# Row panel sums of the first sweep: added by VectorE, or carried on in PSUM from a copy by ScalarE

## What is computed

```python
d = rsqrt(sum(adj, axis=1) + 1e-6)
x = layernorm(x + (d[:, None] * (adj + I) * d[None, :]) @ (x @ W0))      # layer 0
agg = adj @ x                                                             # layer 1
msg = relu(agg @ W_msg.T + b_msg)
x = layernorm(x + gru_cell(msg, x, W_ih, W_hh, b_ih, b_hh))
```

## Time and profile before

| | us |
|---|---|
| median of 3 runs | 1845.35 |
| lowest and highest | 1844.21, 1848.05 |
| profiled execution, its time | 1845.82 |
| its span in the trace | 1844.0 |
| first sweep, to the end of its last product | about 713 |

### The profile page before, as it was taken

The page is one execution under the profiler, slowest core; times in us unless marked ns, Lnnn a source line. Parts: engine busy times, 40 slices in busy tenths (PEclk is TensorE's granted clock), DMA queues, the critical chain, the costliest instruction groups (busy, mean ns, idle before and its releaser), DMA issues.

```text
span 1844.0 us, 16697 instructions
## 1 busy us (share of the span) xinstructions
PE 1696.3 (92%) x6400; PEld 1160.4 (63%) x6400; DVE 1444.7 (78%) x1346; ACT 641.9 (35%) x560; POOL 117.0 (6%) x110
## 2 busy tenths in 40 slices
PE   0088799997999999999999999999999999999996
PEld 0043344443444556888888888888777777777774
DVE  7888899999999966766666655665877888878785
ACT  0000000000000003445454444444665666566562
POOL 0000000000000011200000000000001011110101
PEclk9999999999999999999999999999999999999998
DMA  9999999999999962666566565665998888989891
GB/s 390 422 386 422 420 423 420 421 416 422 384 422 421 420 236 85 205 196 202 195 197 201 192 201 191 198 196 188 384 314 303 299 302 309 311 291 319 286 313 51
DMA packets 180927, 551.10 MB, mean 299 GB/s; under 512 B 13424, under 2 KB 13936, under 8 KB 148080
## 3 DMA queue, kind: packets, MB, share of 16 engines
q1 hardware_dynamic: 177280, 541.11, 79.4%
q0 software_dynamic: 2560, 8.39, 1.3%
q10 hardware_dynamic: 1008, 0.53, 0.1%
HBM read 545.79 MB, written 4.19 MB: 298 GB/s over the span
## 4 chain that ended last, share of the span: by engine, by line
PE 76%; DVE 12%; DMA 9%; issue 2%; ACT 1%; POOL 0%; SPq 0%; DVEq 0%; ACTq 0%; POOLq 0%
PE bank L487 17%; PE bank L489 17%; PE bank L488 17%; PE bank L435 15%; DMA ring<-adj_blocks 6%; DVE colsum L763 5%; DVE feat L767 2%; DVE feat L770 2%; DMA pool<-adj_blocks 2%; DMA kept<-adj_blocks 1%; PE bank L420 1%; PE bank L554 1%; PE bank L567 1%; PE bank L565 1%; PE bank L457 1%
## 5 line engine op out<-in xcount | busy, mean ns | idle before, releaser
L788 DVE TENSOR_TENSOR lo<-ring,hi 128x2048 fp32r<-128x2048 f32 x206 | 470.2, 2289 | 288.9 <-ACT f L653 209.3
L642 ACT ACTIVATE hi<-ring 128x2048 fp32r<-128x2048 f32 x206 | 394.9, 1918 | 396.2 <-DMA ring<-adj_blocks 239.1
L487 PE MATMUL bank<-hi,x1s 128*128 128x512 f32 x1024 | 416.6, 407 | 3.1 <-DVE lo L788 1.9
L489 PE MATMUL bank<-hi,x1s 128*128 128x512 f32 x1024 | 399.2, 390 | 0.0
L488 PE MATMUL bank<-lo,x1s 128*128 128x512 f32 x824 | 321.1, 390 | 0.0
L435 PE MATMUL bank<-kept,feat 128*128 128x512 f32 x600 | 267.9, 597 | 11.6 <-DMA kept<-adj_blocks 11.6
L487 PEld LDWEIGHTS bank<-hi,x1s 128*128 128x128 f32 x1024 | 192.4, 188 | 52.7 <-issue 7.2
L489 PEld LDWEIGHTS bank<-hi,x1s 128*128 128x128 f32 x1024 | 192.3, 188 | 41.2
L435 PEld LDWEIGHTS bank<-kept,feat 128*128 128x128 f32 x600 | 113.2, 191 | 155.4 <-issue 137.5
L763 DVE TENSOR_TENSOR colsum<-colsum,kept 128x2048 f32<-128x2048 f32 x81 | 185.6, 2291 | 9.9 <-DMA kept<-adj_blocks 8.2
L435 PE MATMUL bank<-ring,feat 128*128 128x512 f32 x376 | 173.9, 610 | 16.0 <-DMA ring<-adj_blocks 16.0
(11 more groups left out here) (99 smaller groups left out, 1600.2 us busy)
## 6 DMA issues: line engine op xcount, KB each, us to landing
ring<-adj_blocks SPq DMA_DIRECT2D x412, 512.0 KB, 5.2
kept<-adj_blocks SPq DMA_DIRECT2D x126, 1024.0 KB, 12.3
ring<-adj_blocks SPq DMA_DIRECT2D x85, 1024.0 KB, 12.2
more<-adj_blocks SPq DMA_DIRECT2D x100, 512.0 KB, 6.0
pool<-adj_blocks SPq DMA_DIRECT2D x45, 1024.0 KB, 12.2
xt<-x_t SPq DMA_DIRECT2D x8, 512.0 KB, 12.1
xin<-x POOLq DMA_DIRECT2D x16, 256.0 KB, 3.5
out<-y POOLq DMA_DIRECT2D x16, 256.0 KB, 4.2
```

The costliest lines, as they stand in the source:

```text
L487: pe.matmul(acc[:, :], fh, ah, start=start and c == 0, stop=False, skip_group_check=True)
L489: mm = pe.matmul(acc[:, :], fl, ah, start=False, stop=stop and c == KC - 1, skip_group_check=True)
L642: ins = act.activation(hi[:, n % NHI], raw(slot_of2[n]), ACT.Copy)
L788: ins = dve.tensor_tensor(flat(low(n)), flat(raw(slot_of2[n])), flat(hi[:, n % NHI]).bitcast(f32), ALU.subtract)
```

## The change

Groups from the eighth on no longer start from zero. ScalarE copies the panel's sum so far from `part` into the group's pair of banks (`seed`), and TensorE's products are accumulated onto it (`start` is set for the first eight groups only). When the group ends, ScalarE copies the pair back to `part` (`leave`, for all groups but the last), and then seeds the next but one. TensorE waits for `seeded` where it waited for the add. VectorE's adds go, and its two last ones become copies. The planner has no adds any more, and a longer time from the end of a group until its banks are free.

```diff
-    SUM, SUM_LOW, SUM_FIRST, FOLD, ADD = 0.92, 1.0, 0.8, 0.5, 0.52
-    PRODUCT, SELF, DEGREES, SUPPORT, FEATURE, EVICT, MARGIN = 1.38, 0.72, 0.68, 0.72, 1.9, 0.56, 0.8
+    SUM, SUM_LOW, SUM_FIRST, FOLD = 0.92, 1.0, 0.8, 0.5
+    PRODUCT, SELF, DEGREES, SUPPORT, FEATURE, EVICT = 1.38, 0.72, 0.68, 0.72, 1.9, 1.1
...
-        ready += [(max(now["dve"], t), 0, "add", g) for g, t in ended_groups.items()]
...
-                if g < NP:
-                    left[g] = now["pe"] + EVICT
-                else:
-                    ended_groups[g] = now["pe"] + MARGIN
+                left[g] = now["pe"] + EVICT
...
-            if g < NP:
-                eng.wait_ge(evicted, g + 1)
-            else:
-                eng.wait_ge(added, g + 1 - NP)
+            eng.wait_ge(evicted, g + 1)
...
-                if begins and g >= 2:
+                if begins and g >= NP:
+                    pe.wait_ge(seeded, g - NP + 1)
+                elif begins and g >= 2:
                     group_left(pe, g - 2)
...
-                                       start=begins and u == 0 and j != 4 * P,
+                                       start=begins and g < NP and u == 0 and j != 4 * P,
...
-                              start=begins and c % KC == 0, stop=False, skip_group_check=True)
+                              start=begins and g < NP and c % KC == 0, stop=False, skip_group_check=True)
...
-                    pe.wait_ge(last_added, q + 1)
+                    pe.wait_ge(last_out, q + 1)
...
-            def evict(g):
-
-                R, units = groups[g]
-                act.wait_ge(prod_done, product_no[units[-1]])
+            def leave(t):
+
+
+                g = group_of[t]
+                if groups[g][1][-1] != t or g == len(groups) - 1:
+                    return
+                R = groups[g][0]
+                act.wait_ge(prod_done, product_no[t])
                 for h in range(2):
                     i = 2 * R + h
                     ins = act.activation(part[:, i * W:(i + 1) * W], group_bank(g, h)[:, :], ACT.Copy)
                 ins.then_inc(evicted, 1)
+                if NP <= g + 2 < len(groups):
+                    seed(g + 2)
+
+            def seed(g):
+                R = groups[g][0]
+                act.wait_ge(evicted, g - 1)
+                for h in range(2):
+                    i = 2 * R + h
+                    ins = act.activation(group_bank(g, h)[:, :], part[:, i * W:(i + 1) * W], ACT.Copy)
+                ins.then_inc(seeded, 1)
...
+                for t in before_degrees[P]:
+                    leave(t)
...
                 feature(P)
-                for g in {0: range(0, NP - 1), 1: [NP - 1]}.get(P, []):
-                    evict(g)
+                for t in after_degrees[P] + burst[P]:
+                    leave(t)
...
-            def add_group(g):
-                R, units = groups[g]
-                dve.wait_ge(prod_done, product_no[units[-1]])
-                if g == NP:
-                    dve.wait_ge(evicted, NP)
-                for h in range(2):
-                    rows = part[:, (2 * R + h) * W:(2 * R + h + 1) * W]
-                    ins = dve.tensor_tensor(rows, rows, group_bank(g, h)[:, :], ALU.add)
-                ins.then_inc(added, 1)
...
-                    for g in range(NP, len(groups) - 1):
-                        if add_after[g] == n and n < NT1 - 1:
-                            add_group(g)
...
-            def add_half(h):
+            def half_out(h):
...
-                dve.tensor_tensor(rows, rows, group_bank(g, h)[:, :], ALU.add).then_inc(last_added, 1)
-
-            for g in range(NP, len(groups) - 1):
-                if add_after[g] >= NT1 - 1:
-                    add_group(g)
+                dve.tensor_copy(rows, group_bank(g, h)[:, :]).then_inc(last_out, 1)
+
             split_lo(0)
             split_lo(1)
-            add_half(1)
+            dve.wait_ge(evicted, len(groups) - 1)
+            half_out(1)
             row_step(whole[1])
-            add_half(0)
+            half_out(0)
```

More of the change, by code:

```diff
@@ L95, in gnn_resnorm_kernel @@
     landed, summed, multiplied, left, folded, featured, xt_there, supported = {}, {}, {}, {}, {}, {}, {}, {}
-    holder, slot_of1, before1, add_after, ended_groups = {}, [], [], {}, {}
+    holder, slot_of1, before1 = {}, [], []
     now = {"sp": 0.8, "pe": 0.0, "dve": 0.0}
@@ L165, in gnn_resnorm_kernel @@
                 to_fold = T1[of][0]
-        elif kind == "fold":
+        else:
             now["dve"] = folded[of] = begin + FOLD
             to_fold = None
-        else:
-            now["dve"] = left[of] = begin + ADD
-            add_after[of] = at_sum - 1
-            del ended_groups[of]
     freed_at = {s: max(summed[m], multiplied.get(T1[m], 0)) for s, m in holder.items()}
@@ L336, in gnn_resnorm_kernel @@
         consts, zeroed = sem("consts"), sem("zeroed")
-        fold_done, added, brz_ready = sem("fold_done"), sem("added"), sem("brz_ready")
+        fold_done, brz_ready = sem("fold_done"), sem("brz_ready")
         sum_done, csum_ready, deg_done, deg_ready, dinv_ready = (
             sem("sum_done"), sem("csum_ready"), sem("deg_done"), sem("deg_ready"), sem("dinv_ready"))
-        supp_done, feat0_ready, prod_done, evicted, half_done, last_added = (
-            sem("supp_done"), sem("feat0_ready"), sem("prod_done"), sem("evicted"), sem("half_done"),
-            sem("last_added"))
+        supp_done, feat0_ready, prod_done, evicted, seeded, half_done, last_out = (
+            sem("supp_done"), sem("feat0_ready"), sem("prod_done"), sem("evicted"), sem("seeded"),
+            sem("half_done"), sem("last_out"))
         hi_ready, lo_ready, tile_done = sem("hi_ready"), sem("lo_ready"), sem("tile_done")
```

## The result

| | before | changed kernel |
|---|---|---|
| median, in us | 1847.06 (11 runs, 1844.21 to 1850.52) | 1840.88 (11 runs, 1840.07 to 1843.42) |
| profiled execution, its span | 1844.0 | 1838.9 |
| ratio | | 0.9967 (95% interval 0.9958 to 0.9976) |

The change is worth 6.2 us (by the interval of the ratio 4.4 to 7.8); 6.55 was the sum. The time lies 1.9 us over the 1839.0 that was forecast, mostly because the median of before was taken at 1845.35 from three runs and is 1847.1 with eleven.

The account below looks back on a forecast made before the run. First sweep: DMA, VectorE and TensorE neck and neck; afterwards TensorE alone sets the pace. Waiting 3.25 plus clock 3.30 gives 6.55 us off, median 1845.35 to 1838.8, rounded to 1839; range 1836.5 to 1843.5 us.

Parts of the forecast that it names:

- The place and the cause: End of stage 3, first sweep: VectorE's adds make column sum L775 late, so TensorE waits 3.0 us before the degrees.
- 3.25 us of waiting: Stage 3: without the adds TensorE's degrees start at 451.65 instead of 454.90 us, right behind the product of load 172.
- 3.30 us of clock: Stage 3, degrees to next panel's support: 12.09 instead of 15.39 us, as TensorE's low clock after the wait goes.
- Nothing for ScalarE's share: ScalarE's evictions and seeds, 0.6 us a half, about 2.9 us together, hide beside TensorE's group of 13.7 us: no cost.
- The fold's margin: Column sum L775 of stage 3 would be ready at 449.3 us, 2.3 us before TensorE's degrees could start.
- One to one to the end: After stage 3: later column sums keep up and the second sweep is TensorE-bound, so all 6.55 us reach the end.
- Half of the gain: Rival at stage 3: the wait goes, but the slow stretch doesn't count or a load wait returns it: 1842.1 us; chance 0.15.
- No change: Rival: bunched sums cause VectorE's lag, or seeds cost TensorE what the sums give: 1845 plus or minus 1; chance 0.08.
- Slower by starved loads: Rival, 260 to 448 us: re-planned slots starve the DMA queue; three holes, 12.3 us, give 1851 us; chance 0.05.

Follow-up runs that it names:

- the last set: The changed kernel run again, unaltered, beside new runs of the kernel before on one chip: 1839.52 us, ratio 0.9958.
- blank additions: The changed kernel with 27 pairs of additions of weights into PSUM bank 6 on VectorE, in the places of the old adds: 1850.04 us, ratio 1.0015.
- the filler experiment: The kernel before with four unneeded matmuls on TensorE between the product of load 172 and the degrees of stage 3: 1844.50 us, ratio 0.9987.
- the new slots in the kernel before: The kernel before, VectorE's adds kept, with loads placed in the slots planned for the changed kernel: 1845.34 us, ratio 0.9990.

## Why the prediction was right, and where its numbers were off

**The place and the cause** were right. The wait for L775 was the only one behind 455 us, VectorE was late by its adds, and putting the load back brings the wait and the slow stretch back.

**3.25 us of waiting.** Measured 3.65 in the trace. The missing 0.4 is the landing of load 172 (447.75 for 448.21), which I had taken as fixed "because DMA is full up to there". It was nearly full: 416 for 421 GB/s between 350 and 400 us is 0.6 us, and it stood in the row. The pair of traces of the last set has the same difference, 448.10 and 447.52. The blank additions show that this grows with VectorE's lag.

**3.30 us of clock.** Measured 3.30 in the trace (3.22 in the pair of the last set), 2.8 in the median of the filler experiment and 3.19 in its trace. Right in size, but the reason that I gave ("every wait over two microseconds in this trace was followed by a slow stretch") doesn't hold over more traces, as told below.

**Nothing for ScalarE's share.** Right; 0.6 us a half was 0.592, the hand-over 2.2 us of work and not 2.4.

**The fold's margin.** 2.3 us forecast, 2.5 measured. The fold of stage 5 was forecast for 596.5 and came at 591.9: the hole in DMA after 450 us, which I had carried over into the sum, went away with the change. Its causes are two. TensorE had stood still and then run slowly, holding its slots, and VectorE was late with its sums: where the wait and the slow stretch are nearly gone and VectorE is as late as before (the new slots in the kernel before), DMA moves 408 GB/s from 450 to 500 us, for 387 before and 420 in the changed kernel.

**One to one to the end.** Right up to the second sweep (6.95 us at its first matmul), not in the two traces beyond: the spans differ by 5.1 us. TensorE's waits from 1200 to 1400 us (who for whom: us, times, longest), in the kernel before and in the changed one:

```profile
PE bank L487 <- DVE lo L788: 1.6, 2, 1.0
```

```profile
PE bank L477 <- DVE lo L781: 3.4, 2, 2.8
```

There the sweep goes over from layer 0 to layer 1 and the loads speed up from 195 to 337 GB/s. The prediction read the earlier trace rows as if DMA fell back to the end; from the 29th slice (1290 us) on it is at eight and nine tenths again, and the shift doesn't pass that place unchanged. The longest of these waits is 1.0 us in the first trace of before, but 2.2 in its second, and from 0.9 to 2.9 in the experiments, with no order to it. It looks like a difference of single executions and not of the kernels; why it differs is open. From the start of the second sweep to the end it is 1130.7 us in the first trace of before and 1131.4 to 1132.7 in the other twelve. Medians of eleven runs give 6.2 us, and the last set 8.1; in its two traces the second sweep starts 6.93 us sooner.

**The rivals.** Half of the gain: no, but the clock term is as uncertain as that rival said. No change: no. Slower by starved loads: the mechanism is real, in the other direction. It was VectorE's lag that starved DMA, by 0.6 us in the kernel before and by 2.5 with the blank additions. In the changed kernel the new slots cost nothing; beside VectorE's adds they do starve DMA (408 GB/s from 350 to 400 us, 1.5 us), though the kernel got faster by it.

## What to carry to other kernels

Two engines at 98% of a window can hide which of them is late: compare when the data landed with when the engine took it up, at the one place where a third engine waits for both. A wait that ends at such a join costs its length and, on TensorE, often the half clock behind it, and it disappears as a whole as soon as the late engine has a margin. Once the join is gone, the work of the engine behind it counts in full, and the next gain is to take work from that engine, even onto the one that has just been relieved.

## What the runs showed of the hardware

TensorE's granted clock after a wait is not a function of the wait's length. I took every wait of 1.75 us or more for a load or a column sum between 110 and 500 us from the thirteen traces. Of eight between 1.75 and 2.0 us, two were followed by a slow stretch (a product of 5.4 us instead of 3.7), of thirty between 2.0 and 2.5 us twenty-one were, and of the three of 2.97 us and more all three. A wait of 2.47 to 2.50 us at about 170 us stands in every trace; it brought the slow clock in eight and not in five. Each such stretch costs 1.7 us where products come first and 3.2 to 3.5 us where the degrees do, and is at the lower of the two levels, 1.2 GHz: in the kernel before, the granted clock is 1.00 from 445 to 452 us and 0.50 from 455 to 460.

The Trainium skill (TensorE: Matmul & The Clock Gate, Part 1) says that the moment at which the clock changes depends on windows that run free of the kernel. The traces agree: equal waits have unequal costs. A sum should enter the clock term with the share of executions in which it comes.

A granted clock of 1.00 in a row is no proof of full speed where TensorE does next to nothing. From 50 to 100 us TensorE is busy 3.57 us, and the row says 1.00 in the trace of the kernel before and 0.50 in that of the changed one; the degrees of stage 0 at 92 us take 3.57 us in both, as at the lower level, where 1.84 is the full speed. The mean clock of a whole execution is about 0.97 or about 0.99, in most kernels here both, with no clear difference in the times to match; only within one of the two groups does the mean say something.

ScalarE copies 128x512 float32 into PSUM in 592 ns, as fast as out of it (595), while TensorE writes other banks; the products of 3.43 us don't lengthen. A VectorE copy of 128x512 from PSUM takes 0.69 us, no less than the addition that it replaced (0.69; L743 took 0.68).
